# Reordering the scores, values and maxima inside the attention groups of a fused adaLN transformer block on one Trainium2 core

## The chip, the cores and the metric

The kernel runs on one core of one Trainium2 chip. The metric is the device time of one execution in microseconds, from start to end of the whole program; lower is better. The engines are named as the profile names them: PE (TensorE matmul), PEld (its weight loads), DVE (VectorE), ACT (ScalarE), POOL (GpSimd) and SP (SyncE, which here issues nearly all DMAs).

## The reference

Four sequences of 512 tokens with 256 channels go through one block: a modulated layer norm, causal attention with 32 query heads and 8 key/value heads of width 8, a gated residual, a second modulated layer norm, and a mixture of 16 experts (top 4 within the best 2 of 4 groups) with a shared expert, again with a gated residual.

```python
h = _layernorm(x, axis=-1) * (1 + ca) + sa
x = x + ga * attn(h, wq, wk, wv, wo)
h = _layernorm(x, axis=-1) * (1 + cb) + sb
x = x + gb * ffn(h, gate_w, expert_up_w, expert_down_w, shared_up_w, shared_down_w)
# attn
att = einsum('bhqd,bhkd->bhqk', q, k) / sqrt(8)
att = softmax(where(causal, att, -inf))
y = einsum('bhqk,bhkd->bhqd', att, v);  return y @ wo
# ffn
out = sum_e cw[:, e] * (swiglu(xt @ up[e].T) @ down[e].T) + swiglu(xt @ shared_up.T) @ shared_down.T
```

## The kernel before

Everything is written by hand: each engine has its own instruction list, and semaphores tie them together. The program has three stages: projections of q, k and v with a first set of maxima (to about 71 us), the attention (71 to 356 us), and router, shared expert and routed experts (to the end). The change touches the attention alone.

**The attention** is cut into eight halves `u` (a sequence and 16 of its 32 query heads each). A half has ten groups `n`, one for each pair of a query tile `q` and a key tile `kt` of the causal triangle, in the order (0,0), (1,1), (1,0), (2,2), (2,0), (2,1), (3,3), (3,0), (3,1), (3,2). A group has four slots `g`, one per key head of the half.

What PE does in a half, all of it in the order of `half(u)` in the tensor block:

- `scores(u, n, g)` (L668): one bf16 matmul of 512 columns, scores of one key head against four query heads, into one of **two** PSUM banks, 4 and 5, in turn (`score_bank`). It waits until ACT has taken the exponential of the tile two before it (`st_free`). ACT's exponential (L1085) writes the probabilities to `probs`, which has four slots of a group each.
- `weigh_values(u, m)` (L679), "the values": eight f32 matmuls that multiply the probabilities of an earlier group `m` (two groups back, table `WEIGH`) by V, into bank 6. When the last group of a query tile is weighed, ACT copies bank 6 out (`out_of_psum`, L1070, "a leave" below, table `LEAVE`; four in a half, in groups 1, 2, 4 and 7).
- `scores_for_max(u + 1, q, i)` (L646 and L649), "a pair": scores of the **next** half, into two banks of 0 to 3. DVE takes their row maxima (L1394, `maxima`). There are 22 pairs in a half: 2, 4, 8 and 8 for the query tiles 0 to 3. PE may be two pairs ahead of DVE (`s_free`).
- `turn_max` (L690): a transpose of the finished maxima of one query tile. DVE copies them out (L1400, `take_max`), POOL splits them into three bf16 parts (`split`, L1216 to L1222), and SP writes them as rows into Q (L416, `put_negm`), so that the score matmul of the next half subtracts the maximum by itself.
- `project` (L699) in the last group of halves 2, 4 and 6: the output projection of the sequence finished before, two blocks of eight matmuls. DVE adds the result to X (L1418, L1421, `residual`).

DVE also takes the reciprocal of the row sums (L1404, `invert`) and multiplies the attention output by it (L1408, `normalise`), which waits for a chain of DMAs: SP sends the sums and values out, reads them back, starts the loads of Q and K for the half after the next (L396, L397, `load_half`), then writes the inverse to DRAM (L442) and reads it back spread over partitions (L445). In halves 3 to 6 DVE has pieces of the second layer norm in addition (`NORM_AT`, `SCALE_AT`). POOL masks the four probability tiles of each diagonal group (L1207) and does the splits between them.

Before the change the pairs stand in the slots that `pairs_after` gives: slots 1 and 3 of the groups of query tiles 0, 1 and 3, and in groups 3 to 5 (query tile 2) slots 1, 2 / 0, 1, 3 / 0, 2, 3. The values stand behind the first score of a group. In the last half, u = 7, there are no pairs, the scores use four banks, and parts of the second layer norm's transposes (L747) and the router (L759, L773 to L779) stand between the scores.

Of the kernel before, what the change touches and what calls it, by code (L numbers as in the profile page):

```python
# [20 lines left out]
QT = T // P  # L21
NT = B * QT
GH = NKV // 2
# [46 lines left out]
S_TOT = sum(S_PAIRS.values())  # L70

# [8 lines left out]
def adaln_block(nc, x, wq, wk, wv, wo, gate_t, up_t, down_t, shared_up_t, shared_down_t, c_t, wmod, out):  # L80
# [10 lines left out]
    with ExitStack() as ctx:  # L91
# [203 lines left out]
        def score_bank(u, tile):  # L295
# [5 lines left out]
        NORM_AT = {(0, 0): ("stats", 0), (1, 0): ("stats", 1), (2, 0): ("stats", 2), (2, 2): ("stats", 3),  # L301
                   (3, 0): ("mean", 0),
                   (6, 0): ("centre", 0), (7, 0): ("centre", 1), (7, 2): ("centre", 2), (8, 0): ("centre", 3)}
        SCALE_AT = {(0, 0): 0, (1, 0): 1, (2, 0): 2, (2, 2): 3}

        def pairs_after(q, slot):

            n = (q + 1) * GH
            return range(slot * S_PAIRS[q] // n, (slot + 1) * S_PAIRS[q] // n)
# [59 lines left out]
        with nc.Block() as block:  # L369
# [203 lines left out]
            def _(pe):  # L573
# [129 lines left out]
                def half(u):  # L703
                    for n, (q, kt) in enumerate(GROUPS):
                        for g in range(GH):
                            slot = GH * (n - FIRST[q]) + g
                            scores(u, n, g)
                            if g == 0:
                                back_, m = WEIGH[n]
                                if u - back_ >= 0:  # L710
                                    weigh_values(u - back_, m)
                            if u + 1 < HALVES:
                                for i in pairs_after(q, slot):
                                    scores_for_max(u + 1, q, i)
                            if (n, g) == (0, 2):
                                turn_max(u, QT - 1)
                            elif kt == q and g == 2 and u + 1 < HALVES:
                                turn_max(u + 1, q - 1)
# [252 lines left out]
            def _(act):  # L971
# [106 lines left out]
                def half(u):  # L1078
                    for n, (q, kt) in enumerate(GROUPS):
                        group = NG * u + n  # L1080
                        above(act, s["av_done"], group - SLOTS + 1)
                        for g in range(GH):
# [4 lines left out]
                            if g == 1 and n in LEAVE:  # L1087
                                back_, left = LEAVE[n]
                                if u - back_ >= 0:
                                    out_of_psum(u - back_, left)  # L1090
# [88 lines left out]
            def _(gp):  # L1179
# [112 lines left out]
                for u in range(HALVES):  # L1292
                    for q in range(QT):
                        for g in range(GH):
                            mask(u, FIRST[q], g)
                            if g == 2 and q == 0:
                                split(u, QT - 1)
                            elif g == 2 and u + 1 < HALVES:
                                split(u + 1, q - 1)
# [40 lines left out]
            def _(dve):  # L1340
# [82 lines left out]
                def half(u):  # L1423
                    for n, (q, kt) in enumerate(GROUPS):
                        for g in range(GH):
                            slot = GH * (n - FIRST[q]) + g
                            if u + 1 < HALVES:
                                for i in pairs_after(q, slot):
                                    maxima(u + 1, q, i)
                            if (n, g) == (0, 2):  # L1430
                                take_max(u, QT - 1)
                            elif kt == q and g == 2 and u + 1 < HALVES:
                                take_max(u + 1, q - 1)
                            if u > 0 and (n, g) == (5, 2):
                                invert(u - 1)
                            if u > 0 and (n, g) == (8, 2):
                                normalise(u - 1)
                            if u % 2 == 0 and u > 0 and (n, g) in ((9, 1), (9, 3)):
                                residual(u // 2 - 1, g // 2)
                            if u in (3, 5) and (n, g) in NORM_AT:  # L1440
                                what, i = NORM_AT[n, g]
# [6 lines left out]
                            if u in (4, 6) and (n, g) in SCALE_AT:  # L1448
                                scale_rows(dve, u // 2 - 2, SCALE_AT[n, g])

# [294 lines left out]
```

How the kernel before makes its waits and increments, by code:

```python
        def link(eng, ins):  # L248
            chained[0] += 1
            ins.then_inc(s["chain"], 1)
            eng.wait_ge(s["chain"], chained[0])
# [1 line left out]
        def above(eng, signal, count):  # L254
            if count > 0:
                eng.wait_ge(signal, count)
# [1 line left out]
        def layer_norm(dve, b, to):  # L259
            for i in range(QT):
                st = nc.vector.bn_stats(ln_st[:, i, :], X[:, b * QT + i, :])
            st.then_inc(s["soft"], 1)
            dve.wait_ge(s["soft"], 3 * b + 1)
            for i in range(QT):
                ag = nc.vector.bn_aggr(ln_mv[:, i, :], ln_st[:, i, :])
            ag.then_inc(s["ln_stats"], 1)
            dve.wait_ge(s["ln_sdev"], b + 1)
            nc.vector.reciprocal(ln_rs[:, :], ln_sd[:, :]).then_inc(s["soft"], 2)
            dve.wait_ge(s["soft"], 3 * b + 3)
            above(dve, s["tr_done"], b - 1)
            for i in range(QT):
                last = nc.vector.tensor_scalar(to(i), X[:, b * QT + i, :], ln_mv[:, i, 0:1], ln_rs[:, i:i + 1],
                                               ALU.subtract, ALU.mult)
            last.then_inc(s["xn_ready"], 1)
# [35 lines left out]
        def norm_stats(dve, m, i):  # L311
            if i == 0:
                dve.wait_ge(*((s["x2_ready"], 2 * m + 2) if m < B - 1 else (s["added"], 4)))
            t = m * QT + i
            nc.vector.bn_stats(norm_st[:, t, :], X[:, t, :]).then_inc(s["norm_st"], 1)
# [7 lines left out]
        def centre(dve, m, i):  # L323
            if i == 0:
                dve.wait_ge(s["norm_mv"], m + 1)
            t = m * QT + i
```

## Time and profile before

| what | value |
|---|---|
| time, median of 3 runs | 672.74 us (671.09 to 674.74) |
| profiled execution: its time / its span | 671.22 us / 669.5 us |
| mean granted TensorE clock | 0.944 |
| PE busy | 602.4 us (90%) |
| DVE busy | 395.1 us (59%) |
| ACT busy | 311.7 us (47%) |
| POOL busy | 342.3 us (51%) |
| chain that ended last, by engine | PE 54%, DMA 18%, DVE 11%, SP queue 6%, POOL 4%, ACT 4% |

The span is the time between the first and the last instruction of the profiled execution. A busy share says how long an engine had an instruction in flight; PE's matmuls are pipelined, so its 90% is not 90% of its peak. The chain that ended last is followed back from the last instruction to what released it, and so on; an engine that stands in it set the time there.

### The profile page before, as it was taken

Reading aid. Unit: us, or ns where it says so; the run is one execution under the profiler, and the core shown is the slowest. Engines: PE = TensorE matmul, PEld = TensorE weight load, DVE = VectorE, ACT = ScalarE, POOL = GpSimd, SP = SyncE. Lnnn points to the kernel's source line nnn. Section 1 sums busy time; section 2 is a strip of 40 time slices with the busy share of each in tenths; the row PEclk is TensorE's granted clock in tenths of the full one; section 3 lists DMA queues with packets and bytes.
Section 4 is the critical chain, followed back from the end, with each engine's and each line's share of the span. In section 5 each row is a group of like instructions: output and inputs, shape, how many; then the busy total and the mean of one; then the engine's idle time right before and its main releaser. Section 6 shows DMA issues by size and latency. Waiting matters only on the chain.

```text
span 669.5 us, 11590 instructions
## 1 busy us (share of the span) xinstructions
PE 602.4 (90%) x3416; PEld 342.1 (51%) x3416; DVE 395.1 (59%) x736; ACT 311.7 (47%) x664; POOL 342.3 (51%) x451
## 2 busy tenths in 40 slices
PE   7979899879999999999989999799999999999910
PEld 5445433324443434333534565566777777777710
DVE  5768677747788879897698747023333333333317
ACT  3434577647677766777682332133333333333300
POOL 5016744415273725453457777426656656565630
PEclk8979599989999999999998989989999999999965
DMA  9698459672414141511115999637666676666667
GB/s 278 175 274 197 139 146 298 195 221 41 109 38 111 38 112 20 129 21 38 16 52 162 392 314 325 218 63 115 111 110 112 109 112 115 104 114 109 95 141 273
DMA packets 83688, 96.08 MB, mean 144 GB/s; under 512 B 12250, under 2 KB 76474, under 8 KB 83374
## 3 DMA queue, kind: packets, MB, share of 16 engines
q1 hardware_dynamic: 67006, 73.46, 39.1%
q0 software_dynamic: 14448, 19.80, 18.0%
q10 hardware_dynamic: 2176, 2.10, 0.9%
q8 instruction: 30, 0.49, 0.3%
q14 instruction: 28, 0.23, 0.1%
HBM read 48.63 MB, written 43.65 MB: 138 GB/s over the span
## 4 chain that ended last, share of the span: by engine, by line
PE 54%; DMA 18%; DVE 11%; SPq 6%; POOL 4%; ACT 4%; issue 3%; POOLq 0%; DVEq 0%; ACTq 0%
PE bank L930 12%; PE bank L948 9%; DMA y_inverse<-inverse 5%; PE bank L846 5%; PE bank L679 5%; PE bank L668 4%; PE bank L865 3%; DMA y_sum<-arena 3%; DVE negm L1394 3%; PE bank L918 2%; DMA arena<-y_inverse 2%; PE bank L646 2%; PE bank L939 2%; ACT arena L1085 2%; DMA q_rows<-arena 2%
## 5 line engine op out<-in xcount | busy, mean ns | idle before, releaser
L1394 DVE TENSOR_REDUCE negm<-bank 128x2 f32<-128x1024 f32 (+3 forms) x176 | 192.2, 1119 | 53.4 <-PE bank L649 52.6
L1085 ACT ACTIVATE arena<-bank 128x512 f32<-128x512 f32 x320 | 181.4, 600 | 89.3 <-PE bank L668 83.2
L1329 POOL DMA_INDIRECT y_sum<-arena x79 | 123.2, 1560 | 92.6 <-DVE arena L1691 84.5
L1207 POOL TENSOR_SCALAR_AFFINE_SELECT arena<-arena 128x512 f32<-128x512 f32 x128 | 80.8, 644 | 131.7 <-ACT arena L1085 128.9
L668 PE MATMUL bank<-arena 75*128 75x512 bf16 x320 | 121.0, 396 | 9.2 <-ACT arena L1085 2.8
L930 PE MATMUL bank<-arena 128*128 x316 | 110.0, 471 | 0.3 <-issue 0.3
L646 PE MATMUL bank<-arena 72*128 72x128 bf16 (+2 forms) x384 | 83.3, 279 | 8.5 <-DVE negm L1394 8.5
L649 PE MATMUL bank<-arena 118*128 118x128 bf16 x512 | 84.9, 231 | 3.2 <-DMA arena<-k_rows 3.2
L679 PE MATMUL bank<-arena 128*9 128x512 f32 x640 | 85.4, 606 | 2.4 <-ACT arena L1070 1.3
L1158 ACT ACTIVATE arena<-bank 128x176 f32<-128x176 f32 x79 | 25.0, 317 | 130.1 <-PE bank L930 130.1
L1684 DVE TENSOR_TENSOR arena<-bank,arena 128x176 f32<-128x176 f32 x79 | 27.0, 342 | 93.9 <-ACT arena L1158 93.9
L668 PEld LDWEIGHTS bank<-arena 75*128 75x128 bf16 x320 | 30.7, 99 | 99.1 <-ACT arena L1085 83.2
L948 PE MATMUL bank<-arena 88*128 x316 | 81.2, 379 | 0.0
L1691 DVE TENSOR_SCALAR arena<-bank,arena 128x256 f32<-128x256 f32 x79 | 38.2, 484 | 59.3 <-PE bank L948 53.0
L1323 POOL DMA_INDIRECT x_rows<-arena,slots x64 | 62.9, 983 | 19.4 <-issue 19.4
L930 PEld LDWEIGHTS bank<-arena 128*128 128x128 f32 x316 | 59.1, 193 | 25.9 <-issue 6.2
L649 PEld LDWEIGHTS bank<-arena 118*128 118x128 bf16 x512 | 49.2, 104 | 20.7 <-issue 6.9
L948 PEld LDWEIGHTS bank<-arena 88*128 88x128 f32 x316 | 53.6, 190 | 4.5 <-issue 0.2
L646 PEld LDWEIGHTS bank<-arena 72*128 72x128 bf16 x384 | 38.5, 100 | 33.6 <-DVE negm L1394 23.6
L846 PE MATMUL bank<-arena 128*128 128x512 f32 (+1 forms) x96 | 43.7, 610 | 0.0
L918 PE MATMUL bank<-ident,arena 128*128 128x128 f32 x158 | 31.6, 283 | 5.0 <-DMA arena<-x_rows 5.0
L918 PEld LDWEIGHTS bank<-ident,arena 128*128 128x128 f32 x158 | 20.8, 142 | 29.3 <-issue 12.4
(176 smaller groups left out, 619.2 us busy)
## 6 DMA issues: line engine op xcount, KB each, us to landing
arena<-x_rows SPq DMA_DIRECT2D x79, 144.0 KB, 2.5
arena<-q_rows SPq DMA_DIRECT2D x8, 1200.0 KB, 8.9
q_rows<-arena SPq DMA_DIRECT2D x24, 384.0 KB, 4.4
arena<-up_t SPq DMA_DIRECT2D x2, 2816.0 KB, 20.6
arena<-y_sum SPq DMA_DIRECT2D x8, 512.0 KB, 6.7
arena<-down_t SPq DMA_DIRECT2D x2, 1408.0 KB
x_rows<-arena SPq DMA_DIRECT2D x17, 144.0 KB, 3.4
k_rows<-arena SPq DMA_DIRECT2D x24, 96.0 KB, 3.0
```

The lines of the kernel that those rows point to most:

```text
L646: nc.tensor.matmul(bank[:, buf + j, at_:at_ + n - P], Q[k][0:PR, head, q * P:q * P + P], K[k][0:PR, head // REP, 0:n - P], start=(c == 0), ...
L649: last = nc.tensor.matmul(bank[:, buf + j, at_ + n - P:at_ + n], Q[k][0:MR, head, q * P:q * P + P], K[k][0:MR, head // REP, q * P:q * P + ...
L668: nc.tensor.matmul(bank[:, score_bank(u, tile), :], K[k][0:KR, g, kt * P:kt * P + P], Q[k][0:KR, g * REP:g * REP + REP, q * P:q * P + P], ...
L679: last = nc.tensor.matmul(bank[32 * g:32 * g + VW, OBANK, :], V[:, b * QT + kt, h * GH + g, :], probs[:, (NG * u + n) % SLOTS, g, :], star ...
L846: last = nc.tensor.matmul(bank[0:w, 2 * k + i, :], ws_up[:, c, c0:c0 + w], h2T[n][:, c, :], start=(c == 0), stop=(c == DC - 1))
L918: last = nc.tensor.transpose(bank[:, t % 2, c * P:c * P + P], xt[t % XT][:, c * P:c * P + P], ident[:, :])
L930: last = nc.tensor.matmul(bank[:, 2 + t % 2, 0:2 * I], xT[t % 2][:, c, :], w[:, bass.ds(e * (DC * 2 * I) + c * 2 * I, 2 * I)], start=(c == ...
L948: last = nc.tensor.matmul(bank[:, 6 + t % 2, 0:D], actT[t % 2][0:I2, c, :], w[0:I2, bass.ds(e * D, D)], start=(c == 0), stop=(c == 1))
L1085: nc.scalar.activation(probs[:, group % SLOTS, g, :], bank[:, score_bank(u, tile), :], ACT.Exp, scale=SCALE).then_inc(s["st_free"], 1)
L1207: nc.gpsimd.affine_select(out=block_, in_=block_, compare_op=ALU.is_ge, fill=0.0, base=0, pattern=[[0, REP], [1, P]], channel_multiplier=- ...
L1329: gp.indirect_dma_start(y_sum[t % 2], bass.IndirectOffsetOnAxis(ap=xt[t % XT][:, D:D + 1].bitcast(U32), axis=0), yo[t % YO], None, compute ...
L1394: nc.vector.tensor_reduce(to, view, AX.X, ALU.max, negate=True).then_inc(s["s_free"], 1)
```

## The change

Inside each group of the attention the order on PE becomes: two scores, then the values (and the turn of finished maxima, if there is one), then a pair, two scores, and a pair; a group with three pairs has one between its last two scores as well. The pairs are handed out to the ten groups as 2, 2, 2, 2, 3, 2, 2, 2, 2, 3, where it was 2, 2, 2, 2, 3, 3, 2, 2, 2, 2. The turns stand in slot 1 of groups 0, 1, 3 and 7, where they stood in slot 2 of groups 0, 1, 3 and 6. ACT's leave stands behind the third exponential of its group instead of the second. POOL's split stands behind all four masks of a diagonal group instead of between the third and the fourth. On DVE `invert` moves from slot 2 to slot 1 of group 5, `normalise` from slot 2 to slot 3 of group 8, and the pieces of the second layer norm to slot 1 of groups 0 to 4 and 6 to 9. No instruction is added or removed, and no buffer changes.

```diff
+GROUP_PAIRS = (2, 2, 2, 2, 3, 2, 2, 2, 2, 3)
+ALL_PAIRS = [(q, i) for q in range(QT) for i in range(S_PAIRS[q])]
+PAIRS_OF = [ALL_PAIRS[sum(GROUP_PAIRS[:n]):sum(GROUP_PAIRS[:n + 1])] for n in range(NG)]
+SLOTS_OF = {2: (1, 3), 3: (1, 2, 3)}
+TURN_OF = {0: (0, 3), 1: (1, 0), 3: (1, 1), 7: (1, 2)}
...
-        NORM_AT = {(0, 0): ("stats", 0), (1, 0): ("stats", 1), (2, 0): ("stats", 2), (2, 2): ("stats", 3),
-                   (3, 0): ("mean", 0),
-                   (6, 0): ("centre", 0), (7, 0): ("centre", 1), (7, 2): ("centre", 2), (8, 0): ("centre", 3)}
...
+        NORM_AT = {0: ("stats", 0), 1: ("stats", 1), 2: ("stats", 2), 3: ("stats", 3), 4: ("mean", 0),
+                   6: ("centre", 0), 7: ("centre", 1), 8: ("centre", 2), 9: ("centre", 3)}
...
                     for n, (q, kt) in enumerate(GROUPS):
                         for g in range(GH):
-                            slot = GH * (n - FIRST[q]) + g
                             scores(u, n, g)
-                            if g == 0:
+                            if g == 1:
                                 back_, m = WEIGH[n]
                                 if u - back_ >= 0:
                                     weigh_values(u - back_, m)
+                                if n in TURN_OF and u + TURN_OF[n][0] < HALVES:
+                                    turn_max(u + TURN_OF[n][0], TURN_OF[n][1])
                             if u + 1 < HALVES:
-                                for i in pairs_after(q, slot):
-                                    scores_for_max(u + 1, q, i)
-                            if (n, g) == (0, 2):
-                                turn_max(u, QT - 1)
-                            elif kt == q and g == 2 and u + 1 < HALVES:
-                                turn_max(u + 1, q - 1)
+                                for q_, i in pair_at(n, g):
+                                    scores_for_max(u + 1, q_, i)
...
-                            if g == 1 and n in LEAVE:
+                            if g == 2 and n in LEAVE:
...
-                            if g == 2 and q == 0:
-                                split(u, QT - 1)
-                            elif g == 2 and u + 1 < HALVES:
-                                split(u + 1, q - 1)
+                        if q == 0:
+                            split(u, QT - 1)
+                        elif u + 1 < HALVES:
+                            split(u + 1, q - 1)
...
-                            if u > 0 and (n, g) == (5, 2):
+                            if u > 0 and (n, g) == (5, 1):
                                 invert(u - 1)
-                            if u > 0 and (n, g) == (8, 2):
+                            if u > 0 and (n, g) == (8, 3):
                                 normalise(u - 1)
```

The change moves lines, so a line of the kernel after is 3 to 7 higher than the same line before (L668 is L673, L679 is L684, L649 is L654, L690 is L695, L1085 is L1088, L1394 is L1397, L1408 is L1411).

**PE, group 0 of half 5, before.** L668 is a score, L679 the values, L649 with x7 a pair, L690 the turn.

```order
L668 MATMUL bank<-arena 128x512 [waits st_free,nm_in0]
L679 MATMUL bank<-arena 9x512 [waits st_free]
L679 MATMUL bank<-arena 9x512 x3
L668 MATMUL bank<-arena 128x512 [waits st_free]
L649 MATMUL bank<-arena 128x128 [waits s_free,k_in0,q_in0]
L649 MATMUL bank<-arena 128x128 x7
L668 MATMUL bank<-arena 128x512 [waits st_free]
L690 MATMUL bank<-ident,negm 16x128 [waits misc_free,s_free]
L668 MATMUL bank<-arena 128x512 [waits st_free]
```

The same group after the change:

```order
L673 MATMUL bank<-arena 128x512 [waits st_free,nm_in0]
L673 MATMUL bank<-arena 128x512 [waits st_free]
L684 MATMUL bank<-arena 9x512 [waits st_free]
L684 MATMUL bank<-arena 9x512 x3
L695 MATMUL bank<-ident,negm 16x128 [waits misc_free,s_free]
L654 MATMUL bank<-arena 128x128 [waits s_free,k_in0,q_in0]
L654 MATMUL bank<-arena 128x128 x7
L673 MATMUL bank<-arena 128x512 [waits st_free] x2
```

The second score moved ahead of the values, and the values, the turn and the pair now stand in one row between the second score and the third. The group's second pair follows in both.

**ACT, group 1 of half 1**, which has a leave (L1070), and the first exponential of group 2, before. L1085 is an exponential; the first of a group also waits for `av_done`.

```order
L1085 ACTIVATE arena<-bank 128x512 [waits st_ready,av_done]
L1085 ACTIVATE arena<-bank 128x512 [waits st_ready]
L1070 ACTIVATE arena<-bank 128x4x128 [waits av_done]
L1085 ACTIVATE arena<-bank 128x512 [waits st_ready] x2
L1085 ACTIVATE arena<-bank 128x512 [waits st_ready,av_done]
```

After the change:

```order
L1088 ACTIVATE arena<-bank 128x512 [waits st_ready,av_done]
L1088 ACTIVATE arena<-bank 128x512 [waits st_ready] x2
L1073 ACTIVATE arena<-bank 128x4x128 [waits av_done]
L1088 ACTIVATE arena<-bank 128x512 [waits st_ready]
L1088 ACTIVATE arena<-bank 128x512 [waits st_ready,av_done]
```

The leave moved from ahead of the third exponential to behind it.

**DVE, the end of half 3**, before: L1394 is the maxima of a pair, L1408 `normalise`, L327 and L336 pieces of the second layer norm.

```order
L1394 TENSOR_REDUCE negm<-bank 128x2 [waits s_ready]
L327 SCALAR_TENSOR_TENSOR arena<-X,norm_mv,gate_bc 128x256
L1394 TENSOR_REDUCE negm<-bank 128x2 [waits s_ready]
L1408 TENSOR_TENSOR arena<-arena 128x512 [waits y_in0]
L1394 TENSOR_REDUCE negm<-bank 128x2 [waits s_ready] x3
L336 SCALAR_TENSOR_TENSOR arena<-arena,norm_rs,gate_bc 128x256 [waits centred,inverse_sd]
```

After the change:

```order
L1397 TENSOR_REDUCE negm<-bank 128x2 [waits s_ready]
L1411 TENSOR_TENSOR arena<-arena 128x512 [waits y_in0]
L1397 TENSOR_REDUCE negm<-bank 128x2 [waits s_ready]
L332 SCALAR_TENSOR_TENSOR arena<-X,norm_mv,gate_bc 128x256
L1397 TENSOR_REDUCE negm<-bank 128x2 [waits s_ready] x2
L1403 COPY arena<-bank 16x128 [waits nm_split,misc_ready]
```

In both, three maxima of the half stand behind `normalise`. Their pairs stand on PE in slot 3 of group 8 and slots 1 and 3 of group 9 before, and in slots 1, 2 and 3 of group 9 after; one piece of the layer norm moved in between, and the copy of the turned maxima moved ahead of the next half's first maxima.

## Rows read from the trace of the kernel before

**Rows 1.** Who waited for whom, whole span: total us, times, longest.

```profile
ACT arena L1085 <- PE bank L668: 83.2, 97, 5.6
PEld bank L668 <- ACT arena L1085: 83.2, 145, 0.9
...
DVE arena L1408 <- DMA arena<-y_inverse: 10.3, 5, 5.3
```

**Rows 2.** Stretches by half (0 to 5): us, busy and instructions, PEclk, DMA, GB/s.

```profile
71.70:106.90 35.20, 33.83 (x224) 15.02 (x226) 23.80 (x26) 24.00 (x44) 19.19 (x36) 0.84 0.67 165
106.90:145.90 39.00, 32.09 (x240) 12.76 (x236) 25.69 (x29) 24.38 (x44) 16.52 (x37) 0.98 0.78 245
145.90:184.60 38.70, 37.30 (x256) 16.51 (x252) 27.83 (x32) 24.39 (x44) 15.42 (x32) 0.93 0.39 99
184.60:217.90 33.30, 31.39 (x240) 12.52 (x236) 28.59 (x41) 24.29 (x45) 17.13 (x34) 1.00 0.34 75
217.90:254.90 37.00, 35.09 (x256) 15.51 (x252) 30.32 (x37) 24.32 (x45) 15.82 (x32) 1.00 0.31 68
254.90:287.70 32.80, 31.37 (x240) 12.53 (x236) 28.57 (x41) 24.28 (x45) 17.09 (x34) 1.00 0.34 76
```

**Rows 3.** Timeline of group 1 of half 3: start us, us, engine, instruction.

```profile
188.55 0.39 PE L668 MATMUL bank<-arena 75*128 75x512 bf16 x1
...
188.97 0.60 ACT L1085 ACTIVATE arena<-bank 128x512 f32<-128x512 f32 x1 [0.64 <-PE bank L668]
...
189.24 0.38 PE L668 MATMUL bank<-arena 75*128 75x512 bf16 x1
...
189.47 0.59 ACT L1070 ACTIVATE arena<-bank 128x512 f32<-128x512 f32 x1
...
189.63 0.39 PE L668 MATMUL bank<-arena 75*128 75x512 bf16 x1
...
189.94 1.75 ACT L1085 ACTIVATE arena<-bank 128x512 f32<-128x512 f32 x3
...
190.61 0.39 PE L668 MATMUL bank<-arena 75*128 75x512 bf16 x1
```

**Rows 4.** Timeline of PE, the values of half 3 (groups 0, 1, 2, 8, 9) and next.

```profile
184.45 1.05 PE L679 MATMUL bank<-arena 128*9 128x512 f32 x8
187.57 1.04 PE L679 MATMUL bank<-arena 128*9 128x512 f32 x8
190.93 1.05 PE L679 MATMUL bank<-arena 128*9 128x512 f32 x8
...
210.67 1.05 PE L679 MATMUL bank<-arena 128*9 128x512 f32 x8
213.71 1.04 PE L679 MATMUL bank<-arena 128*9 128x512 f32 x8
217.73 1.05 PE L679 MATMUL bank<-arena 128*9 128x512 f32 x8
```

**Rows 5.** Chain that ended last, in group 0 of half 3: start us, us.

```profile
186.27 0.22 PE bank L668
186.49 0.11 PE bank L690
```

**Rows 6.** Timeline of DVE, first maxima behind normalise of half 3.

```profile
215.69 3.48 DVE L1394 TENSOR_REDUCE negm<-bank 128x2 f32<-128x1024 f32 x3
```

**Rows 7.** Timeline of SP's queue, half 3: load of Q, read of inverse.

```profile
201.64 0.90 SPq L396 DMA_DIRECT2D arena<-q_rows  x1
...
211.79 0.58 SPq L445 DMA_DIRECT2D arena<-y_inverse  x1
```

**Rows 8.** Timeline of PE, the end of half 1.

```profile
144.35 0.50 PE L646 MATMUL bank<-arena 72*128 72x384 bf16 x1 [4.76 <-DVE negm L1394]
```

**Rows 9.** Stretch behind it, columns as in rows 2.

```profile
144.00:150.00 6.00, 5.65 (x27) 2.20 (x28) 3.58 (x4) 1.70 (x3) 1.27 (x2) 0.51 0.97 344
```

**Rows 10.** Timeline of DVE in half 7: the router's first step.

```profile
332.92 0.22 DVE L1497 TENSOR_REDUCE few<-rt 128x4 f32<-128x64 f32 x1 [0.57 <-ACT rt L1076]
```

More of the change, by code:

```diff
@@ L297, in score_bank, with pair_at @@
             return 4 + tile % 2 if u < HALVES - 1 else (4, 5, 0, 1)[(tile - E_TOT * u) % 4]
-        NORM_AT = {(0, 0): ("stats", 0), (1, 0): ("stats", 1), (2, 0): ("stats", 2), (2, 2): ("stats", 3),
-                   (3, 0): ("mean", 0),
-                   (6, 0): ("centre", 0), (7, 0): ("centre", 1), (7, 2): ("centre", 2), (8, 0): ("centre", 3)}
[L304 to L309, printed above, removed]
+        NORM_AT = {0: ("stats", 0), 1: ("stats", 1), 2: ("stats", 2), 3: ("stats", 3), 4: ("mean", 0),
+                   6: ("centre", 0), 7: ("centre", 1), 8: ("centre", 2), 9: ("centre", 3)}
+        def pair_at(n, g):
+            slots_ = SLOTS_OF[GROUP_PAIRS[n]]
+            return [PAIRS_OF[n][slots_.index(g)]] if g in slots_ else []
         def norm_stats(dve, m, i):
@@ L1423, in half @@
                 def half(u):
-                    for n, (q, kt) in enumerate(GROUPS):
+                    for n in range(NG):
                         for g in range(GH):
-                            slot = GH * (n - FIRST[q]) + g
+                            if g == 1 and n in TURN_OF and u + TURN_OF[n][0] < HALVES:
+                                take_max(u + TURN_OF[n][0], TURN_OF[n][1])
                             if u + 1 < HALVES:
-                                for i in pairs_after(q, slot):
+                                for q, i in pair_at(n, g):
                                     maxima(u + 1, q, i)
[L1430 to L1433, printed above, removed]
-                            if u > 0 and (n, g) == (5, 2):
+                            if u > 0 and (n, g) == (5, 1):
                                 invert(u - 1)
-                            if u > 0 and (n, g) == (8, 2):
+                            if u > 0 and (n, g) == (8, 3):
                                 normalise(u - 1)
@@ L1439, in half @@
                                 residual(u // 2 - 1, g // 2)
-                            if u in (3, 5) and (n, g) in NORM_AT:
-                                what, i = NORM_AT[n, g]
+                            if u in (3, 5) and g == 1 and n in NORM_AT:
+                                what, i = NORM_AT[n]
                                 if what == "stats":
@@ L1447, in half @@
                                     centre(dve, u // 2 - 1, i)
-                            if u in (4, 6) and (n, g) in SCALE_AT:
-                                scale_rows(dve, u // 2 - 2, SCALE_AT[n, g])
+                            if u in (4, 6) and g == 1 and n < QT:
+                                scale_rows(dve, u // 2 - 2, n)
                 count = [0]
```

## The prediction

> **What bounds the kernel now.** I read the waits first: ACT waits 83.2 us for the scores (L668), in 97 waits, and the weight loads of the scores wait just as long for ACT's exponentials (L1085) [rows 1]. Two engines that wait for each other point to a loop through the two score banks. So the attention is to be read as a cycle, not by busy shares. The stretches by half give its length: 33.3 us in half 3, 37.0 in half 4, and PE busy nearly throughout [rows 2]; half 5 is like half 3 with 32.8 us. Half 4 is longer than half 3 for its output projection.
>
> The timeline of one group shows the cycle's parts [rows 3]. From the start of a score to its exponential it takes 188.97 - 188.55 = 0.42 us. ACT starts its next instruction 0.50 and 0.47 us after the one before (188.97, 189.47, 189.94), say 0.49. From the start of an exponential to the score that may use its bank: 189.63 - 188.97 = 0.66 and 190.61 - 189.94 = 0.67. The second score and a pair take PE 189.24 - 188.55 = 0.69; a score alone is 0.22 and a turn 0.11 [rows 5], so a pair is 0.47. The values start 190.93 - 190.61 = 0.32 behind their score and hold PE for 188.55 - 187.57 = 0.98 [rows 3, 4].
>
> With these the old cycle closes. Values, second score and pair, exponential of the third score, release of its bank, first score of the next group: 0.98 + 0.69 + 0.42 + 0.66 + 0.32 = 3.07 us; group 8 took 213.71 - 210.67 = 3.04. With a leave the path runs through ACT: 0.98 + 0.42 + 0.49 + 0.49 + 0.66 + 0.32 = 3.36; group 1 took 190.93 - 187.57 = 3.36 [rows 4]. The third exponential ends it, and the fourth is free time: its bank is wanted only behind the values, 0.98 us later. That is what the old order hides.
>
> **The change, part by part.** The same instructions run, so every term is a wait.
>
> *Values behind the second score.* The second score needs the bank of the previous group's **fourth** exponential, and the values stand behind it. The new cycle: 0.98 values, 0.47 pair, 0.42 to the third exponential, 0.49 to the fourth, 0.66 until its bank is free, 0.32 to the values: 3.34 us instead of 3.07. ACT has two tiles to work on beside the values, about 1.1 us, but then idles until the third score, and no tile is ready for it.
>
> *Leave behind the third exponential.* It now stands between the third and the fourth, both on the cycle: + 0.49, so 3.83 instead of 3.36. Before it filled ACT's idle time in part.
>
> *Turn.* It stood beside a wait for a bank and cost nothing; now it stands in the cycle: + 0.11 in groups 0, 1, 3 and 7. Its cover was PE's wait for the fourth score.
>
> *Pairs of query tile 2* write 768 columns instead of 1024, so 0.35 instead of 0.47 by that ratio: - 0.12 in groups 3 to 6. The third pair of group 4 lies behind the fourth score, beside ACT's work.
>
> Groups 0 to 8 of a half: 9 x 3.34 + 4 x 0.49 + 4 x 0.11 - 4 x 0.12 = 31.98 us. In half 3 they took 213.71 - 184.45 = 29.26 [rows 4]. So **+ 2.7 us**.
>
> *Group 9 with three pairs.* Its third pair needs the maxima of its first. From the values on: 0.98, then about 0.6 from a pair to its maxima (no row gives it better than the pair's 0.47 and the engine step of 0.1 to 0.2), about 1.2 for them (three take 3.48 [rows 6]), the third pair 0.47, a score 0.22, the next and the values 0.54: 4.0 us. Before it took 217.73 - 213.71 = 4.02 in half 3, and 0.5 less in half 5 if its other groups are alike [rows 2, 4]: part of it was the wait for `normalise`, whose inverse is read 211.79 - 201.64 = 10.2 us behind the load of Q [rows 7]. As the groups before grow, this wait is covered. In halves 4 and 6 the two projections fill PE and only the moved pair counts. I take + 0.1 for a half, with 0 and 0.9 as ends.
>
> *Start of the next half.* The turn in group 0 needs the third maxima, which end some 1.6 + 3.5 = 5.1 us behind group 9's values; PE gets there at 4.0 + 0.98: + 0.3 with DVE's other work (ends 0 and 0.7).
>
> Halves 3 to 6: 4 x (2.7 + 0.1 + 0.3) = **+ 12.4**.
>
> *Halves 0 and 1.* At the end of half 1 PE waits 4.76 us for maxima behind `normalise` [rows 8]; the DMA chain that ends there begins with a split in group 3 of half 0. What groups grow behind it is swallowed: half 1 about 3.1, half 0 about 2 (its groups 0 and 1 have no values). The chain itself starts later by what groups 0 to 2 of half 0 grow, less the turn's earlier slot: + 0 to + 2.5. I take **+ 1.0**.
>
> *Half 2.* It grows by 3.1 too. But behind the 4.76 us of standing still the granted clock is 0.51 from 144 to 150 us [rows 8, 9], the 1.2 GHz level, and the mean of halves 0 and 2 is lower than that of the others [rows 2]. Half 2 took 38.7 us, half 4 with the same work 37.0 [rows 2], so the slow clock costs 1.7. With the wait mostly covered I take that back: **+ 1.4** (ends 1.4 and 3.1).
>
> *Half 7.* No pairs, four score banks, and from its third group on a chain on DVE. Its router exponential stood behind a leave; now the leave is behind it. DVE waited only 0.57 us for it [rows 10], which is all there is to win: **- 0.5**.
>
> *At nothing:* POOL's later split (the rows it makes are wanted half a half later, or gate the load, within the 0 to 2.5 above); the layer norm's pieces on DVE, which is busy 28.6 of 33.3 us; `invert` a pair earlier, since its write queues behind the load anyway; SP's DMAs keep their order. Behind 356 us nothing changes.
>
> Sum: 12.4 + 1.0 + 1.4 - 0.5 = **+ 14.3 us**. The profiled execution took 671.22 us, so 685.5; the median of the runs shown, 672.74, is 1.5 us above it, and on it the sum gives 687.0 us. From the ends: at least 4 x 2.7 + 0 + 1.4 - 0.5 = + 11.7; I take off 3 more for parts of the cycle that may be shorter, so + 9. At most 4 x 4.3 + 2.5 + 3.1 - 0.5 = + 22.
>
> **The rivals.**
>
> *A, PE's clock falls more often.* It fell where PE had stood still for 4.76 us [rows 8, 9], and the new order adds 0.3 to 0.8 us of waiting to every group. One fall for each of the halves 1 to 6 at 1.7 us each, on top: 10 more, 697 us. Against it: in halves 3 to 5 the clock stays at 1.00, though PE waits there in every group [rows 2], and no added wait is near 4.76 us.
> The Trainium skill ("TensorE: Matmul & The Clock Gate", the section on a second HAM failure mode, PSUM-queue depth-cycling) says that small idle gaps of PE between groups of matmuls, from cycling through PSUM banks, can make the clock swing between both levels. By that rule this order would pay here; this trace has such gaps at clock 1.00 and does not show it.
>
> *B, the ends of halves swallow more.* If DMA chains kept the end of halves 3 to 6 where it is, each would grow only by the excess over its wait: half 3 waits 4.02 - 3.04 = 1.0 us there, half 5 0.5, and halves 4 and 6 perhaps as much. At most 3 in all less, and halves 0 and 1 at nothing: 14.3 - 3 - 1 = + 10.3, about 683 us. The chains start in group 3, so half of it is the more likely.
>
> *C, faster: PE becomes the bound.* The exponentials of the first two tiles run beside the values, and if ACT's banks came free by the time PE is back, a group would cost only PE's own time: four scores, values, two pairs, 4 x 0.22 + 0.1 + 0.98 + 0.94 = 2.90 us, against 3.07 and 3.36. That is 6 x 0.17 + 4 x 0.46 = 2.9 us a half, some 18 in six halves: 655 us. It decides at the second score: from the third score PE needs 0.22 + 0.22 + 0.47 + 0.22 = 1.13 us to come there, the fourth exponential's bank is free after 0.42 + 0.49 + 0.66 = 1.57. The parts would have to be 0.44 us shorter than the rows show.
>
> *D, no difference.* ACT's one idle time moves from behind the first score to behind the second, and what is lost there is won by PE not waiting at the fourth score: 672.7 us. The same two sums speak against it.
>
> **How the numbers follow.** Forecast 0.78; A 0.08; B 0.07; C 0.04; D 0.03. All but C and D are slower by over 0.5% (3.4 us, about what a measurement of this kernel can tell from no change): slower 0.93, same 0.03, faster 0.04. The forecast is 687.0 us. Its own range is + 9 to + 22, 682 to 695; B lies in it, and a little of A is taken in at the top, and below a margin for the terms that are estimates: 679 to 698.
>
> **What would show it.** Right: the values of a group without leave follow each other in 3.3 us, with leave in 3.8, groups 0 to 8 of half 3 take about 32 us; PE waits for L1088 before the second score of each group; ACT idles about 1.1 us once a group, before the third exponential; half 1's end waits little, and the clock stays at 1.00 from there. Behind the attention the time is as before. The prediction is wrong if groups keep 3.04 and 3.36 us (D), drop below 3 (C), or if the granted clock is below 1 in halves 3 to 6 (A).

## The result and the profile after

The change makes the kernel slower: 683.38 us median of 4 runs (680.31 to 689.09) against 673.74 (4 runs of before), a ratio of 1.014 (95% interval 1.008 to 1.020). A second measurement, on another chip, gave 1.0168 (1.0115 to 1.0221). The forecast was 687.0 us, the range 679 to 698.

The stretches by half of the kernel after, columns as in rows 2, halves 1 to 6:

```profile
109.00:145.10 36.10, 32.36 (x237) 12.77 (x236) 25.94 (x29) 23.76 (x45) 16.34 (x37) 1.00 0.76 242
145.10:184.00 38.90, 35.60 (x253) 15.77 (x252) 28.07 (x32) 23.75 (x44) 15.20 (x32) 1.00 0.40 103
184.00:220.00 36.00, 32.34 (x237) 12.76 (x236) 29.59 (x42) 23.75 (x44) 17.13 (x34) 1.00 0.31 69
220.00:259.70 39.70, 35.75 (x253) 15.78 (x252) 30.88 (x36) 23.75 (x44) 15.76 (x32) 1.00 0.29 63
259.70:295.70 36.00, 32.28 (x237) 12.77 (x236) 29.60 (x42) 23.76 (x44) 17.14 (x34) 1.00 0.32 69
295.70:335.40 39.70, 35.74 (x253) 15.77 (x252) 30.88 (x36) 23.78 (x45) 15.76 (x32) 1.00 0.12 25
```

Halves 3, 4 and 5 took 33.3, 37.0 and 32.8 us [rows 2] and take 36.0, 39.7 and 36.0. PE does the same work, but its busy time in half 3 is 32.34 of 36.0 us, where it was 31.39 of 33.3. Half 7 starts at 335.4 us instead of 323.8 (first exponentials at 335.37 and 323.83). That is **+ 11.5 us**, and 11.5 of 672.7 is a ratio of 1.017. Half 1 became shorter, 36.1 instead of 39.0, and its clock and that of half 2 are now 1.00.

The values of half 3, PE's timeline after, for groups 0, 1, 2, 3, 8, 9 and the next half:

```profile
184.09 1.05 PE L684 MATMUL bank<-arena 128*9 128x512 f32 x8
187.59 1.05 PE L684 MATMUL bank<-arena 128*9 128x512 f32 x8
191.74 1.05 PE L684 MATMUL bank<-arena 128*9 128x512 f32 x8
195.56 1.05 PE L684 MATMUL bank<-arena 128*9 128x512 f32 x8
...
212.88 1.04 PE L684 MATMUL bank<-arena 128*9 128x512 f32 x8
216.19 1.05 PE L684 MATMUL bank<-arena 128*9 128x512 f32 x8
220.08 1.05 PE L684 MATMUL bank<-arena 128*9 128x512 f32 x8
```

A group without leave and turn (group 8) takes 216.19 - 212.88 = 3.31 us, one with a leave (group 2) 195.56 - 191.74 = 3.82. Before, group 8 took 3.04 [rows 4], and group 2, whose values started at 190.93, ended at the values of group 3:

```profile
194.36 1.05 PE L679 MATMUL bank<-arena 128*9 128x512 f32 x8
```

which is 3.43 us. Groups 0 to 8 take 32.10 us, where they took 29.26.

The timeline of group 1 of half 3 after, engines PE and ACT, answers to rows 3:

```profile
187.59 1.05 PE L684 MATMUL bank<-arena 128*9 128x512 f32 x8
188.79 0.28 PE L695 MATMUL bank<-ident,negm 128*16 128x128 f32 x1
...
189.37 0.59 PE L673 MATMUL bank<-arena 75*128 75x512 bf16 x2
189.79 0.60 ACT L1088 ACTIVATE arena<-bank 128x512 f32<-128x512 f32 x1 [1.35 <-PE bank L673]
...
190.28 0.59 ACT L1073 ACTIVATE arena<-bank 128x512 f32<-128x512 f32 x1
190.44 0.39 PE L673 MATMUL bank<-arena 75*128 75x512 bf16 x1
190.76 1.68 ACT L1088 ACTIVATE arena<-bank 128x512 f32<-128x512 f32 x3
191.42 0.39 PE L673 MATMUL bank<-arena 75*128 75x512 bf16 x1 [0.59 <-ACT arena L1088]
```

Read it from the top: values, turn and pair (189.37 is the third score), the third exponential 0.42 us behind its score, the leave 0.49 behind it, the fourth exponential 0.48 behind that (190.76), and 0.66 later, at 191.42, the second score of the next group, which PE waited for. ACT stood idle for 1.35 us before the third exponential; it was 0.64 [rows 3], and about 1.1 was expected. Each step has the length that it had before; only their order on the cycle is new.

Behind the attention the profiled execution of after lost another 6 us. In the chain that ended last POOL's indirect DMAs (L1326) now have 9% of the span: the 64 writes of the routed rows start at the same distance from half 7 as before, but the chain now runs through them and not through PE's shared expert, and the routed experts start 1.4 us later against half 7. Nearly all of the other 4.9 us is in the routed experts, whose instructions are the same in every kernel here; that stretch took 198.8 us in before and 203.4 in after, and, in the experiments below, 200.9 in v2, 203.3 in v1 and 205.5 in v5. These are single executions, and the numbers do not follow the order of the attention, so I put none of it down to the change. Below the kernels are compared by the start of half 7 (323.8 in before, 335.4 in after), which leaves that scatter out, and the ratio stands beside it. One scatter is left in it: the first exponential of half 0 comes at 71.7 us in before and 71.1 in after, and between 70.2 and 72.9 in the other runs. From it to half 7 before takes 252.1 us and after 264.3, so the attention up to half 7 grew by 12.2 us; where the difference matters, this length is given too.

### The profile page after: what moved, and what is told of

Read it like the earlier page. It is cut to its first block, busy times and chain, and to the rows that moved or that the text cites. A ratio compares the mean times of both kernels' runs of the same rounds, so it can differ in the third digit from the quotient of the medians.

```text
span 687.3 us, 11589 instructions
## 1 busy us (share of the span) xinstructions
PE 605.4 (88%) x3416; PEld 341.1 (50%) x3416; DVE 399.1 (58%) x736; ACT 307.5 (45%) x664; POOL 343.0 (50%) x451
## 4 chain that ended last, share of the span: by engine, by line
PE 50%; DMA 13%; ACT 10%; POOL 10%; DVE 8%; issue 6%; SPq 2%; DVEq 0%; POOLq 0%; ACTq 0%
PE bank L933 9%; POOL x_rows L1326 9%; PE bank L684 9%; ACT arena L1088 8%; PE bank L951 7%; PE bank L673 7%; DMA y_sum<-arena 4%; DVE negm L1397 4%; DMA arena<-x_rows 4%; PE bank L651 4%; PE bank L654 3%; PE bank L921 2%; ACT arena L1073 2%; PE bank L942 2%; DMA arena<-k_rows 1%
## 5 line engine op out<-in xcount | busy, mean ns | idle before, releaser
L1397 DVE TENSOR_REDUCE negm<-bank 128x2 f32<-128x1024 f32 (+3 forms) x176 | 192.4, 1120 | 57.5 <-PE bank L654 57.0
L1088 ACT ACTIVATE arena<-bank 128x512 f32<-128x512 f32 x320 | 176.9, 598 | 108.2 <-PE bank L673 104.6
L673 PE MATMUL bank<-arena 75*128 75x512 bf16 x320 | 111.2, 395 | 20.4 <-ACT arena L1088 12.0
L654 PE MATMUL bank<-arena 118*128 118x128 bf16 x512 | 84.0, 227 | 3.3 <-DMA arena<-k_rows 3.3
L684 PE MATMUL bank<-arena 128*9 128x512 f32 x640 | 85.8, 608 | 1.2 <-ACT arena L1073 1.2
L1326 POOL DMA_INDIRECT x_rows<-arena,slots x64 | 63.6, 994 | 19.4 <-issue 19.4
L673 PEld LDWEIGHTS bank<-arena 75*128 75x128 bf16 x320 | 28.8, 100 | 61.0 <-ACT arena L1088 47.9
L654 PEld LDWEIGHTS bank<-arena 118*128 118x128 bf16 x512 | 47.8, 102 | 15.5 <-issue 5.9
```

The costliest lines, as they stand in the source:

```text
L654: last = nc.tensor.matmul(bank[:, buf + j, at_ + n - P:at_ + n], Q[k][0:MR, head, q * P:q * P + P], K[k][0:MR, head // REP, q * P:q * P + ...
L673: nc.tensor.matmul(bank[:, score_bank(u, tile), :], K[k][0:KR, g, kt * P:kt * P + P], Q[k][0:KR, g * REP:g * REP + REP, q * P:q * P + P], ...
L684: last = nc.tensor.matmul(bank[32 * g:32 * g + VW, OBANK, :], V[:, b * QT + kt, h * GH + g, :], probs[:, (NG * u + n) % SLOTS, g, :], star ...
L1088: nc.scalar.activation(probs[:, group % SLOTS, g, :], bank[:, score_bank(u, tile), :], ACT.Exp, scale=SCALE).then_inc(s["st_free"], 1)
L1326: gp.indirect_dma_start(x_rows, bass.IndirectOffsetOnAxis(ap=slots[:, t, k:k + 1], axis=0), rows[:, t, :], None).then_inc(s["rows_out"], 16)
L1397: nc.vector.tensor_reduce(to, view, AX.X, ALU.max, negate=True).then_inc(s["s_free"], 1)
```

## Experiments

The two theories. **Two banks:** a score waits for the exponential two tiles earlier; the values behind the second score put the fourth exponential on the cycle, and whatever ACT does between the third and the fourth with it. **Rivals:** the values' place alone; the leave's place alone; the spread of the pairs with DVE as the bound.

### v1: only the values behind the second score

```diff
 # kernel before
-                            if g == 0:
+                            if g == 1:
                                 back_, m = WEIGH[n]
```

> The kernel before with one edit: the values stand behind the second score of a group (leave, turns, pairs, split and DVE order as before). Two-bank theory: every group without a leave goes from 3.07 to 3.34 us; in a group with one the leave fits into ACT's idle time beside values and pair, so it falls from 3.36 to about 3.34. Groups 0 to 8 of half 3 about 29.6 us (29.26 before), halves 3 to 6 each + 0.3 or a little less, the whole + 1 to + 3 us, ratio 1.002 to 1.005. Rival 'the values' place is all of it': groups 0 to 8 grow by 2 us or more as in the change, the whole + 10 us, ratio 1.014.

Measured: ratio 0.999 (0.9955 to 1.0026), half 7 starts at 324.8. The values of groups 7, 8 and 9 of half 3, PE's timeline:

```profile
207.99 1.04 PE L679 MATMUL bank<-arena 128*9 128x512 f32 x8
211.30 1.05 PE L679 MATMUL bank<-arena 128*9 128x512 f32 x8
214.61 1.05 PE L679 MATMUL bank<-arena 128*9 128x512 f32 x8
```

Group 7 has a leave, group 8 has none, and both take 3.31 us. Groups 0 to 8 take 29.5 us (29.6 expected). The cycle is as long as worked out, and by itself it is nearly free: what it costs the groups without a leave, those with one nearly get back. From the first exponential to half 7 this run takes 252.8 us, 0.7 more than before. The ratio lies below the 1.002 to 1.005 expected, and its interval just reaches it.

### v2: only the leave behind the third exponential

```diff
 # kernel before
-                            if g == 1 and n in LEAVE:
+                            if g == 2 and n in LEAVE:
```

> The kernel before with one edit: ACT's leave stands behind the third exponential instead of the second. Two-bank theory: with the values behind the first score the fourth exponential is not on the cycle, so the leave costs nothing there; the third exponential comes 0.49 us earlier and the next values then wait for the leave: 0.98 + 0.69 + 0.42 + 0.49 + 0.66 = 3.24 us or a little more in groups with one, against 3.36. Groups 0 to 8 of half 3 28.6 to 29.2 us; what they win the wait for normalise at the end of the half takes back; the whole - 2 to 0 us, ratio 0.997 to 1.000. Rival 'the later leave costs by itself': + 0.49 in four groups of a half, + 2 us a half, + 12 us in all, ratio 1.018.

Measured: ratio 0.9945 (0.9899 to 0.9991), half 7 at 325.6; groups 0 to 8 of half 3 28.9 us. Half 7 starts 1.8 us later than in before, and the groups are not the reason. Behind a short wait at the end of half 5 the granted clock fell, which it did not do there in before; the wait on PE and the stretch behind it:

```profile
287.17 0.34 PE L646 MATMUL bank<-arena 72*128 72x384 bf16 x1 [1.22 <-DVE negm L1394]
```

```profile
288.00:292.00 4.00, 4.00 (x27) 1.63 (x27) 2.51 (x4) 1.61 (x3) 1.27 (x2) 0.61 0.00 0
```

The leave's place costs nothing either while the values stand behind the first score. Neither half of the pair costs what the two cost together.

### v3: the change with the leave taken back

```diff
 # kernel after
-                            if g == 2 and n in LEAVE:
+                            if g == 1 and n in LEAVE:
```

> The changed kernel with one edit taken back: the leave behind the second exponential again. Two-bank theory: the leave then runs in ACT's idle time (values end about 1.4 us behind the second score, the third exponential comes at 2.19), so the groups with one fall from 3.8 to about 3.34 (+ 0.11 with a turn): groups 0 to 8 of half 3 about 2 us shorter than the change's 31.8, halves 3 to 6 together - 7 to - 8 us, start of half 7 at about 326 us (335.4 in the change, 323.8 before); ratio to before 1.002 to 1.006. Rival 'the values' place is all of it': nothing falls, half 7 starts at 335, ratio 1.014.

Measured: ratio 1.0047 (1.0006 to 1.0088), half 7 at 330.9. Groups 0 to 8 of half 3 30.4 us, 1.7 less than in the change; halves 3 to 6 together 145.4 us instead of 151.4. So the late leave is 6.0 us of the change in these four, nearly the 7 to 8 expected. The start of half 7 fell only by 4.5, not by 9: the first exponential came 0.9 us later in this execution, and from it to half 3 the run took 113.5 us, where the change took 112.9, so halves 0 to 2 gave nothing. The wait on PE at the end of half 1, and the stretch behind it:

```profile
144.99 0.50 PE L651 MATMUL bank<-arena 72*128 72x384 bf16 x1 [3.40 <-DVE negm L1397]
```

```profile
144.00:150.00 6.00, 5.01 (x24) 1.90 (x25) 3.66 (x5) 1.09 (x2) 1.23 (x2) 0.57 1.09 386
```

With shorter groups the wait for `normalise` at the end of half 1 is back, and so is a granted clock near the 1.2 GHz level behind it, which the change did not have. A gain ahead of that wait is given back there.

This run also prices what is neither the values nor the leave. Halves 3 to 6 took 139.2 us in before, 139.8 in v1 and 145.4 here. So of the + 12.2 us in these halves the late leave is 6.0, the place of the values alone 0.6, and the other 5.6 belong to the turns, the spread of the pairs, POOL's split and DVE's new order. v4 takes the pairs out of them.

### v4: the change with the third pair back in group 5

```diff
 # kernel after
-GROUP_PAIRS = (2, 2, 2, 2, 3, 2, 2, 2, 2, 3)
+GROUP_PAIRS = (2, 2, 2, 2, 3, 3, 2, 2, 2, 2)
```

> The changed kernel with the third pair back in group 5, two pairs in group 9. Two-bank theory: group 9 of an odd half falls from 4.17 to about 3.4 us, group 5 grows by 0.2 to 0.5, since its third pair waits for maxima; odd halves - 0.4 to - 0.9, even halves 0 to - 0.3 (projections fill PE), start of half 7 at 332 to 334 us, ratio to before 1.008 to 1.012. Rival 'the spread of the pairs is the cause, DVE bounds the halves': odd and even halves fall back to 33.3 and 37.0 us, half 7 starts at 324.

Measured: half 7 at 331.8, 3.6 earlier, of which 1.0 is an earlier first score; ratio 1.0179 (1.0091 to 1.0266), too wide to tell from the change. The values of groups 5, 6, 9 of half 3 and 0 of half 4:

```profile
200.70 1.04 PE L684 MATMUL bank<-arena 128*9 128x512 f32 x8
204.12 1.04 PE L684 MATMUL bank<-arena 128*9 128x512 f32 x8
...
214.65 1.05 PE L684 MATMUL bank<-arena 128*9 128x512 f32 x8
217.96 1.05 PE L684 MATMUL bank<-arena 128*9 128x512 f32 x8
```

Group 9 falls from 3.89 us (not 4.17, as the expectation had it) to 3.31, group 5 rises from 3.21 to 3.42. The moved pair costs 2 to 3 us in all, 2.0 of them in halves 3 to 6. From values to values odd halves take 35.5 us and even ones 39.2, where the change has 36.0 and 39.7: the spread of the pairs is a small part, and it does not bound the halves. That leaves 3.6 of the 5.6 us above. No run takes the turns, the split and DVE's order out one by one; the prediction's terms for the turns and the start of the next half, 4 x (0.44 + 0.3) = 3.0, come near it.

### v8 and v9: both orders with half of each exponential

```diff
-                            nc.scalar.activation(probs[:, group % SLOTS, g, :], bank[:, score_bank(u, tile), :], ACT.Exp,
+                            w = T if u in (0, HALVES - 1) else T // 2
+                            nc.scalar.activation(probs[:, group % SLOTS, g, 0:w], bank[:, score_bank(u, tile), 0:w], ACT.Exp,
```

> The order of before, but in halves 1 to 6 the exponential covers only columns 0 to 255 of its 512; the other columns of the probabilities keep what half 0 left there, so the attention's output is not the reference's. Two-bank theory: the step from one exponential to the next falls from 0.49 to about 0.28 us and the release of a bank from 0.66 to about 0.45, so a group without a leave falls from 3.04 to PE's own 2.90 us, and one with a leave from 3.36 to about 2.94. Rival 'the spread of pairs and DVE': both orders stay as they are, since DVE's work is the same.

> The changed order, with the same halved exponentials in halves 1 to 6 (the same columns are left out). Two-bank theory: 0.32 + 0.98 + 0.47 + 0.42 + 0.28 + 0.45 = 2.92 us for a group without leave or turn, the same as the old order beside it, where the full exponential had 3.34 against 3.07; with a leave 3.41. So the groups without a leave no longer differ between the orders by more than 0.1 us, and groups 0 to 8 together by about 2 us less turn, all of it in the groups with a leave or a turn. Rival 'what PE does between the values costs, banks or not': the difference of 0.3 us in groups without a leave stays.

Both kernels leave out columns 256 to 511 of each exponential in halves 1 to 6.

The values of groups 0, 8 and 9 of half 3, in v8 (the old order):

```profile
185.71 1.05 PE L679 MATMUL bank<-arena 128*9 128x512 f32 x8
...
211.23 1.04 PE L679 MATMUL bank<-arena 128*9 128x512 f32 x8 [0.29 <-issue]
214.07 1.05 PE L679 MATMUL bank<-arena 128*9 128x512 f32 x8
```

and in v9 (the changed order), with those of groups 2 and 3 between them:

```profile
185.25 1.05 PE L684 MATMUL bank<-arena 128*9 128x512 f32 x8
...
192.34 1.05 PE L684 MATMUL bank<-arena 128*9 128x512 f32 x8
195.73 1.05 PE L684 MATMUL bank<-arena 128*9 128x512 f32 x8
...
211.10 1.05 PE L684 MATMUL bank<-arena 128*9 128x512 f32 x8
213.99 1.04 PE L684 MATMUL bank<-arena 128*9 128x512 f32 x8
```

Groups 0 to 8 take 28.36 and 28.74 us. The orders differ by 0.4 us, where they differ by 2.8 with whole exponentials. PE's and DVE's instructions are those of before and after; only ACT's are shorter. The sums alone flatter the result: v8 was expected at 2.90 and 2.94 us a group, about 26 us for the nine, and took 28.36, because in the old order some values now wait for something else, those of group 3 for POOL's masks:

```profile
195.52 1.05 PE L679 MATMUL bank<-arena 128*9 128x512 f32 x8 [0.78 <-POOL arena L1208]
```

The clean comparison is group 8, which has neither a leave nor a turn, and at whose end the values wait for nothing in either run: 214.07 - 211.23 = 2.84 us in v8 and 213.99 - 211.10 = 2.89 in v9, where whole exponentials gave 3.04 and 3.31. So in a plain group what the order costs is ACT's step and release time on the cycle. A group with a leave still takes 3.39 in the changed order (3.41 expected). v8 as a whole gained nothing, 676.2 us in its one run: half 3 still took 33.1 us, since `normalise` waits for the DMA at its end.

### v5, v6, v7, v10: the wait at the ends of the halves

v5 moves the inverse ahead of the load on SP; v6 does this and puts the leave behind the first exponential; v7 has the leave alone; v10 is the changed kernel with v5's edit.

```diff
-                    elif u + 2 < HALVES:
-                        sp.wait_ge(s["st_ready"], E_TOT * u)
-                        ...
-                        load_half(u + 2)
-                    if u > 0:
-                        spread_inverse(u - 1)
+                    else:
+                        spread_inverse(u - 1)
+                        if u + 2 < HALVES:
+                            sp.wait_ge(s["st_ready"], E_TOT * u)
+                            ...
+                            load_half(u + 2)
 # v6 and v7
-                            if g == 1 and n in LEAVE:
+                            if g == 0 and n in LEAVE:
```

> The kernel before with one edit on SP: the inverse is written and read back (spread_inverse) ahead of the load of Q and K for the half after the next, instead of behind it. If the wait for normalise at the ends of halves 1 and 3 to 5 is the inverse's write queueing behind that 1.2 MB load, it goes: half 1 about 4.7 us shorter, half 2 another 1.7 by the clock that no longer falls, halves 3, 5 about 1.0 and 0.5, even halves up to 0.4; start of half 7 at 315 to 318 us instead of 323.8, the whole 665 to 667 us, ratio 0.988 to 0.991. Rival 'the load is then late': the load now ends some 3 us later and the first pair of the next half waits for it: half 7 starts at 322 or later, ratio 0.996 or more.

> As v5_inverse_first, and ACT's leave behind the first exponential of its group instead of the second. The leave then starts when the values end, in ACT's idle time before the second exponential, and the groups with one fall from 3.36 to about 3.1 us: another 0.6 to 1.0 us a half, now that no wait at the ends takes it back. Start of half 7 at 311 to 314 us, the whole 660 to 664 us, ratio 0.981 to 0.987. Rival: a leave so early waits for the values and holds up the second exponential, and nothing is won over v5_inverse_first.

> The kernel before with only the leave behind the first exponential. Groups with one fall from 3.36 to about 3.25 us as in the combined run, but the wait for normalise at the end of the halves grows by as much, since the load and the inverse behind it start no earlier: start of half 7 at 322 to 324.5 us (323.8 before), ratio 0.995 to 1.002. Rival 'each group saved is saved at the end': 3 to 4 us less at the start of half 7.

> The changed kernel with SP's inverse ahead of the load, the edit that took 7.6 us off the start of half 7 in the order before. Theory: in the changed order the longer groups already cover the inverse's way in every half, so there is no wait for normalise left to take away: start of half 7 at 334 to 336 us as in the change (335.4), ratio to before 1.008 to 1.020. Rival 'the inverse's chain bounds the halves in both orders': it falls by 5 us or more here too.

| run | ratio to before (95%) | start of half 7, us |
|---|---|---|
| v5, inverse first | 0.9881 (0.9826 to 0.9935) | 316.3 |
| v6, inverse first and leave early | 0.9851 (0.9794 to 0.9908) | 312.4 |
| v7, leave early | 0.9986 (0.9945 to 1.0028) | 323.7 |
| v10, change with inverse first | 1.0188 (1.0124 to 1.0252) | 334.6 |

SP's queue in half 3 of v5, its write, its read and the load:

```profile
198.45 0.33 SPq L442 DMA_DIRECT2D y_inverse<-inverse  x1
199.90 0.56 SPq L445 DMA_DIRECT2D arena<-y_inverse  x1
200.50 0.91 SPq L396 DMA_DIRECT2D arena<-q_rows  x1
```

The small write returns after 199.90 - 198.45 = 1.45 us. In before it is issued behind the load, in half 3 at

```profile
204.82 0.35 SPq L442 DMA_DIRECT2D y_inverse<-inverse  x1
```

and the read follows at 211.79 [rows 7], 7.0 us later. DVE's wait of 10.3 us in five times [rows 1] is gone from the list, half 1 takes 33.4 us instead of 39.0, and its clock and that of half 2 read 1.00. All this took 7.6 us off, as expected (8.5 us from the first exponential to half 7, 243.6 instead of 252.1). On top of it v6 starts half 7 another 3.9 us earlier, but 1.7 of them are an earlier first exponential; the early leave wins the other 2.2, and the two ratios are not clear of each other. Without v5's edit it wins nothing (v7): its groups are shorter, the waits at the ends longer, and behind two of them, of 1.04 and 1.08 us, the granted clock reads 0.74 (216 to 220 us) and 0.78 (288 to 292). In the changed order the same edit wins nothing (v10): the longer groups had covered that wait. v6 is the fastest version measured, 1.5% below before and, by both ratios (0.985 and 1.014), about 3% below the change.

### v11: the change once more

> The changed kernel once more, to fix the size: the stretch to the start of half 7 at 335 us again (+ 11.5), and behind it what the profiled runs scatter by; ratio to before 1.012 to 1.022. Theory and rivals agree here; if half 7 shows the low clock again, that part of its length is the order's, if not it was this one execution's.

Ratio 1.0168 (1.0115 to 1.0221). On this chip, which also ran v7 and v10, before took 715.8 us: the stretch between attention and routed experts is 40 to 45 us longer in all three profiled kernels, for a cause that stays open. In the attention, halves 3 to 6 took 36.0, 39.7, 36.0, 39.7 us again. Half 7 had no low clock here. In the first execution it had, in the second of these stretches, without any long wait of PE in the first:

```profile
349.00:356.00 7.00, 6.37 (x51) 2.97 (x49) 6.61 (x20) 5.04 (x12) 1.50 (x3) 1.00 0.13 42
356.00:363.00 7.00, 7.00 (x30) 2.52 (x30) 5.04 (x16) 4.25 (x10) 5.58 (x6) 0.54 0.25 76
```

v3 showed it in half 7 as well, v4, v10 and v11 did not. Nor does it belong to the new order: v1 has 0.58 from 344 to 348 us, and v5, with the order of before, has

```profile
336.00:340.00 4.00, 4.00 (x16) 0.69 (x15) 3.92 (x10) 2.31 (x5) 2.66 (x3) 0.57 0.01 2
```

So it comes in some executions of both orders, and it is no fixed cost of the change.

## Why the prediction was right, step by step

| step | predicted | measured |
|---|---|---|
| group without leave or turn / with a leave | 3.34 / 3.83 us | 3.31 / 3.82 |
| groups 0 to 8 of half 3 | 31.98 us | 32.10 |
| halves 3 to 6 | + 12.4 us | + 12.2 |
| halves 0 and 1 | + 1.0 | - 0.2 |
| half 2 | + 1.4 | + 0.2 |
| half 7, to the first routed row | - 0.5 | 0.0 |
| behind the attention | 0 | + 1.4, and scatter |

**The cycle** held term by term: the timeline after shows 0.42, 0.49, 0.48 and 0.66, and v8 and v9 show in a plain group that these ACT terms are the difference between the orders. What I had not seen is how far the two parts depend on each other: I wrote of the values and of the leave as two terms with prices of their own (0.27 and 0.49 a group). v1 shows that the first alone is worth nothing within its interval (0.6 us in halves 3 to 6), v2 that the second alone costs nothing (its interval ends just below 1), and the 0.49 exists only with the values behind the second score.

**The turn** was given 0.11. Group 1 took 4.15 us, 0.2 more than 3.34 + 0.49 + 0.11: the turn there needs the maxima of group 0's last pair, and DVE comes late with them. They end at 187.54 + 1.20 = 188.74, and the turn's weights follow:

```profile
187.54 1.20 DVE L1397 TENSOR_REDUCE negm<-bank 128x8 f32<-128x1024 f32 x1
188.79 0.09 PEld L695 LDWEIGHTS bank<-ident,negm 128*16 128x16 f32 x1 [1.08 <-DVE negm L1397]
```

The term was right in kind; the start-of-half term of 0.3 was meant for group 0, and part of it lies in group 1.

**Halves 0 and 1** came out 1.2 us better than forecast. The growth was swallowed whole: the wait of 4.76 us is gone, and the half's own groups now end it at 145.1 us, where the DMA chain had ended it at 145.9. The term that was mis-sized is the "later start of the chain", taken as 1.0. The read at the chain's end and `normalise` in after:

```profile
138.74 0.60 SPq L450 DMA_DIRECT2D arena<-y_inverse  x1
142.08 0.69 DVE L1411 TENSOR_TENSOR arena<-arena 128x512 f32<-128x512 f32 x1 [0.15 <-DMA arena<-y_inverse]
```

In before the read started at 139.10 us. Counted from the first exponential that is 67.6 us now and 67.4 then, so the chain came 0.2 later and not 1.0, and DVE's wait for it shrank from 5.3 us [rows 1] to 0.15.

**Half 2** was mis-sized in its growth, not in the clock. The clock stayed at 1.00, as forecast. Beside the 37.0 us of half 4 it grew by 1.9, to 38.9, and not by the 3.1 that I gave every half; its groups 0 and 1 are 0.7 us shorter than those of half 4, and half 1 ahead of it has no layer norm on DVE.

**The sum.** Up to half 7 the terms made + 14.8; the halves measured + 12.2, and + 11.5 at the start of half 7, since the first score came 0.6 us earlier in that execution. The runs gave + 9.6 us, and + 12 of 715.8 by the second ratio. So the terms of the halves are 2.6 us too high, 2.4 of it at the edges (halves 0 to 2), which I had priced between bounds and not from a cycle; half 7, where the 0.5 to be won did not come, takes 0.5 of that back, and the whole sum of + 14.3 is 2.1 above the + 12.2. Against the first measurement it is 4.7 too high, which also holds the scatter ahead of and behind the attention. In halves 3 to 6 the sum hides an exchange: group 9 was taken at + 0.1 in each and came out at - 0.1, - 0.5, + 0.4 and + 0.3, and the starts of halves 4 and 6 took more than the 0.3 given. That these cancel to 0.2 us is luck; that groups 0 to 8 agree is not.

**Rival A**, the clock: it went the other way in halves 1 and 2, where the fall vanished with the wait. The Trainium skill ("TensorE: Matmul & The Clock Gate", PSUM-queue depth-cycling) tells of a kernel in which small idle gaps between groups of matmuls made the clock swing between both levels; here PE's gaps grew to about 0.6 us in a group, and in halves 1 to 6 the granted clock is 1.00. But one reason that I gave against the rival does not hold, that no added wait is near 4.76 us: the clock also fell behind 1.22 us (v2), 1.12 (v6), 1.04 and 1.08 (v7), and 1.36 (v9, 0.61 from 218 to 222 us), and it stayed at 1.00 behind 1.03 (before, at 129.65 us) and 1.27 (v9, at 291.88). So that the clock held is measured, not explained, and the falls in half 7, which come in both orders, stay open too. **Rival B** holds in halves 0 and 1, and a little in halves 3 and 4, whose last group is 0.1 and 0.5 us shorter than before. **Rival C** fell as worked out: PE waits 0.59 us at the second score. **Rival D** fell with the first row of the group lengths.

## What to carry to other kernels

Where two engines hand two buffers back and forth, write the cycle down step by step and see which handover ends it: a long instruction belongs behind the handover that is not on it, and two moves that are free alone can be dear together. Before shortening groups, look at what ends the stage; a small write queued behind a large load on one DMA queue set it here, and until it was moved the gains ahead of it (v3, v7) came back as a wait, with a slower PE clock behind.

## What the hardware showed that I had not expected

- The granted clock fell to 0.57 behind a wait of PE of 3.40 us (v3) and to 0.51 behind one of 4.76 [rows 8, 9]; removing the wait at the end of half 1, by longer groups or by v5, removed the fall behind it. It also fell behind some waits of 1.04 to 1.36 us (v2, v6, v7, v9) and not behind others of 1.03 and 1.27, so the length of the one wait does not decide it.
- A 32 KB write returned 1.45 us after its issue on an idle queue, and 7.0 us after it behind a 1.2 MB load that was issued 3.2 us earlier on the same queue.
- The routed experts' stretch, with the same instructions, took from 198.8 to 205.5 us in before, after, v1, v2 and v5, more than most of the edits here are worth; halves 3 to 6 of the changed order took 36.0, 39.7, 36.0 and 39.7 us in after and again in v11.
